# Third layer's edge phase: sigmoid and its products with the edge scalar issued one step sooner, second features in a ring of four buffers

## Chip, cores and metric

The kernel runs on one core of one Trainium2 chip. The metric is the device time of one execution in microseconds (us). Before the change it took 13953.59 us as the median of three runs (13917.46 to 13966.27).

## What is computed

Four graph-network layers over 6250 nodes and 100000 edges, float32 throughout. The change lies in the edge phase of the third layer (`_L2_gnn_ref` of the reference). Cut to what matters, with `s` for 64 scalars and `v` for 32 three-vectors of an edge:

```python
w1 = rbf @ W_rbf
m1_s, m1_v = _cg_tp(msg_s, msg_v, y0, y1, *split(w1))   # messages: products with y0, y1
a = sum(leaky(m1_s @ W_alpha) * alpha_dot)               # attention logit
val_s, val_v = m1_s @ Ws_val, einsum(m1_v, Wv_val)
val_v = val_v * sigmoid(val_s @ Wg)[..., None]           # gate
val_s = sigmoid(val_s)
m2_s, m2_v = _cg_tp(val_s, val_v, y0, y1, w2...)         # second product: val_s*y0, dot(val_v, y1), ...
hs, hv = m2_s @ Ws_vlin, einsum(m2_v, Wv_vlin)           # stored per edge
```

`_cg_tp` multiplies scalars by the edge scalar `y0` and by the edge vector `y1`, and takes the dot and cross products of vectors with `y1`.

## The kernel before

The edges are padded to 784 columns of 128. `layer2_edges` (L1917) works on items of four columns (TM = 4, 512 edges), 196 items in all (NM). All engines run the same software pipeline: `steps` (L84) calls a body per step n, and the body handles item n - s for each stage number s. The first and last steps are written out and the middle is a loop over four unrolled steps. The order on each engine is the order of the code, and engines meet only by semaphores. The stages are named in L1918:

- Stage 0: SyncE loads indices and edge features, GpSimd gathers eight blocks of rows (`pool_gather`, L731): four of `gs`, then four of `gd`.
- JOIN 1, PRODUCT 2: VectorE adds `gs` and `gd` to `msg` (L2095) and forms the first features `F` (`dve_message_products`, L629). Its instruction at L644 waits until the four quarters of the item that had this `F` buffer before have been transposed; `F` has two buffers.
- TURN 3: TensorE transposes each of the four quarters of `F` (L677), ScalarE copies them to `FT` (L707), TensorE multiplies by the weights (L658 to L660) and ScalarE copies the result to `O` (L713). The multiplication follows its transposes by two quarters.
- CROSS 5: VectorE finishes the attention logit and the cross product in `O`.
- SECOND_IN 6: ScalarE takes the sigmoid of 96 columns of `O` into the second features `F2` (L1993) at the head of its step, and multiplies 64 of them by `y0`, a quarter at a time, as the last ScalarE instruction of each of the four quarters of that step (`sigmoids_y0`, L1983). The fourth one raises `second_in`. VectorE multiplies the vectors by the gate (L2090) and forms the dot product (L2108, L2123).
- TURN2 7: TensorE transposes `F2` (L677, two blocks a quarter), ScalarE copies to `FT2` (L707, 256 columns), TensorE multiplies (L698, L699), ScalarE copies to `O2` (L720, L721), one of the two with a factor `y0`. For this path there is one PSUM buffer for the transposes and one for the products, so the transposes of a quarter wait until ScalarE has copied those of the quarter before.
- CROSS2 9, LAST 10: VectorE adds the second cross product (L596), SyncE stores.

On each quarter k ScalarE's order is: FT, O, FT2, O2, product with `y0`. TensorE's order is: three transposes, the first multiplication, two transposes of `F2`, the second multiplication; after quarter 1 come the eight matmuls of the edge weights (L2038). At the head of a step TensorE waits, before any of its work:

```python
if m := i_of(TURN):
    wait_apart(pe, sem("products"), m[0] + 1, passed)
if m := i_of(TURN2):
    wait_apart(pe, sem("products2"), m[0] + 1, passed)
    wait_apart(pe, sem("second_in"), m[0] + 1, passed)
```

Since SECOND_IN is 6 and TURN2 is 7, the `second_in` that TensorE's step n + 1 needs is raised by the last ScalarE instruction of step n. `F2` has two buffers, and `prod`, `dot` and `lk` are scratch arrays of VectorE.

Of the kernel before, what the change touches and what calls it, by code (L numbers as in the profile page):

```python
# [585 lines left out]
def comp(ap, n=3):  # L586

    return ap.rearrange("p t (d c) -> p t d c", d=n)
# [1327 lines left out]

def layer2_edges(nc, W, D, logits):  # L1917
    JOIN, PRODUCT, TURN, CROSS, SECOND_IN, TURN2, CROSS2, LAST = 1, 2, 3, 5, 6, 7, 9, 10  # L1918
    RING = 4
    with ExitStack() as ctx:  # L1920
        S = Names(nc, ctx, "e2")
# [7 lines left out]
        ix = [S.sb(f"ix{u}", [P, 2, TM], I32) for u in range(2)]  # L1929
        gs, gd, msg = pair("gs", [P, TM, CX]), pair("gd", [P, TM, CX]), S.sb("msg", [P, TM, MSG_W])  # L1930
        nine = S.sb("nine", [P, TM, NINE_W])
        prod, dot = S.sb("prod", [P, TM, C1V]), S.sb("dot", [P, TM, C1])
        F, F2 = pair("F", [P, TM, X_W]), pair("F2", [P, TM, F2_W + C1])
        FT, FT2 = S.sb("FT", [P, TM, X_W]), S.sb("FT2", [P, TM, F2_W])
        tmp = S.sb("tmp", [P, 3, TM, C1V])
        LIN, VEC, O_W, O2_W = 160, 164, 292, 288
        O, O2 = ([S.sb(f"{name}{u}", [P, TM, w]) for u in range(RING)] for name, w in (("O", O_W), ("O2", O2_W)))
        lk, lsum = S.sb("lk", [P, TM, 64]), S.sb("lsum", [P, TM, 4])
        psW, psF, psO = S.ps("psW", [P, TM, 256]), S.ps("psF", [P, 3, 512]), S.ps("psO", [P, 3, 512])
        parts = ((F[0], 384), (F[1], 384), (F2[0], ET - 768))  # L1940
        starts = (0, 384, 768)
# [35 lines left out]
        @block.scalar  # L1977
        def _(act):
            act.wait_ge(sem("y"), 2 * len(parts))

            def times_y0(to, src, i, k):

                return nc.scalar.activation(to[:, k, :], src[:, k, :], ACT.Copy, scale=y0_of(i, k))  # L1983

            def body(i_of_ring):
                i_of = by_two(i_of_ring)

                def sigmoids():
                    if m := i_of_ring(SECOND_IN):
                        i, u, j = m  # L1990
                        act.wait_ge(sem("lin_O"), (i + 1) * TM)
                        wait(act, sem("lin2_turned"), (i - 1) * TM)
                        nc.scalar.activation(F2[u % 2][:, :, F_B:F_B + C0 + C1], O[u][:, :, 64:160], ACT.Sigmoid).then_inc(sem("sig"), 1)  # L1993

                def sigmoids_y0(k):
                    if m := i_of(SECOND_IN):
                        i, u, j = m
                        if k == 0:
                            act.wait_ge(sem("sig"), i + 1)
                        done = times_y0(F2[u][:, :, F_A:F_A + C0], F2[u][:, :, F_B:F_B + C0], i, k)  # L2000
                        if k == TM - 1:
                            done.then_inc(sem("second_in"), 1)

                sigmoids()
                for k in range(TM):
                    if m := i_of(TURN):
                        act_move(nc, act, m[0], k, FT, psF[:, k % 2, :], S, "lin")
                    if m := two_behind(i_of_ring, TURN, k):
                        i, u, j, n = m
                        if n == 0:  # L2010
                            wait(act, sem("gated"), i - RING + 1)
                            wait(act, sem("logit"), i - RING + 1)
                        act_result(nc, act, i, n, O[u], psO[:, n % 2, :], O_W, S, "lin")
                    if m := i_of(TURN2):
                        act_move(nc, act, m[0], k, FT2, psF[:, 2, :], S, "lin2", F2_W)
                    if m := two_behind(i_of_ring, TURN2, k):
                        i, u, j, n = m
                        if n == 0:
                            wait(act, sem(f"stored{u}"), j * 16)
                        act_result_y0(nc, act, i, n, O2[u], psO[:, 2, :], y0_of(i, n), S, "lin2")  # L2020
                    sigmoids_y0(k)

            steps(act, NM, LAST, body, RING)

        @block.tensor
        def _(pe):
            passed = sem("pe_passed")

            def body(i_of_ring):
                i_of = by_two(i_of_ring)  # L2030

                def weights():
                    if m := i_of(JOIN):
                        i, u, j = m
                        wait_apart(pe, sem(f"es{u}"), (j + 1) * 32, passed)
                        wait_apart(pe, sem("products"), i, passed)
                        for k in range(TM):
                            last = nc.tensor.matmul(psW[:, k, 0:224], es[u][:, P * k:P * k + P], W["l2_rbf"][:, :], start=True, stop=True)  # L2038
                        last.then_inc(sem("weights"), 1)
# [6 lines that stand above are left out]
                for k in range(TM):  # L2046
                    if m := i_of(TURN):
                        i, u, j = m
                        pe_turn(nc, pe, i, k, F[u], psF[:, k % 2, :], W["ident"], S, "lin", 2)
                    if m := two_behind(i_of, TURN, k):  # L2050
                        i, u, j, n = m
                        pe_message_maps(nc, pe, i, n, FT, psO[:, n % 2, :], W, "l2", 96, S, "lin", 2)
                    if m := i_of(TURN2):
                        i, u, j = m
                        pe_turn(nc, pe, i, k, F2[u], psF[:, 2, :], W["ident"], S, "lin2", 1, 2)
                    if m := two_behind(i_of, TURN2, k):
                        i, u, j, n = m
                        pe_maps_y0(nc, pe, i, n, FT2, psO[:, 2, :], W, S, "lin2", 1)
                    if k == 1:
                        weights()  # L2060
# [5 lines left out]
        def _(dve):  # L2066
# [10 lines left out]
            def body(i_of_ring):  # L2077
                i_of = by_two(i_of_ring)
                if m := i_of(PRODUCT):
                    i, u, j = m  # L2080
                    wait(dve, sem("products"), i)
                    dve_message_products(nc, dve, i, psW, msg, nine, dot, F[u], Y3(i), S, (sem("lin_turned"), (i - 1) * TM))
                if m := i_of(SECOND_IN):

                    i, u, j = m
                    dve.wait_ge(sem("sig"), i + 1)
                    dve.wait_ge(sem("cross_done"), i + 1)
                    wait(dve, sem("lin2_turned"), (i - 1) * TM)
                    V2 = comp(F2[u][:, :, F2_X:F2_X + C1V])
                    tt(V2, comp(O[i_of_ring(SECOND_IN)[1]][:, :, VEC:VEC + C1V]), bcast(F2[u][:, :, F2_W:F2_W + C1], 2, 3), ALU.mult).then_inc(sem("gated"), 1)  # L2090
                if m := i_of(JOIN):
                    i, u, j = m
                    dve.wait_ge(sem(f"gathered{u}"), (j + 1) * 16 * 2 * TM)
# [2 lines left out]
                if m := i_of_ring(CROSS):  # L2096
# [4 lines left out]
                    a = O[u][:, :, 0:64]  # L2101
                    nc.vector.scalar_tensor_tensor(out=lk[:, :, :], in0=a, scalar=0.0, in1=bcast(W["l2_adot"][:, :], 1, TM), op0=ALU.max,
                                                   op1=ALU.mult).then_inc(sem("leaky"), 1)
                if m := i_of(SECOND_IN):
                    i, u, j = m
                    dve.wait_ge(sem("gated"), i + 1)
                    wait(dve, sem("products2"), i)
# [1 line left out]
                if m := i_of_ring(CROSS):  # L2109
# [7 lines left out]
                        .then_inc(sem("summed"), 1)  # L2117
                    dve.wait_ge(sem("cross_first"), i + 1)
                    tt(C, C, comp(tmp[:, 0, :, :]), ALU.add).then_inc(sem("cross_done"), 1)
                if m := i_of(SECOND_IN):  # L2120
                    i, u, j = m
                    dve.wait_ge(sem("prod2"), i + 1)
                    nc.vector.tensor_reduce(F2[u][:, :, F_D:F_D + C1], prod[:, :, :].rearrange("p t (d c) -> p t c d", d=3), AX.X,  # L2123
# [712 lines left out]
```

## Time and profile before

| | us |
|---|---|
| median of three runs | 13953.59 |
| profiled execution, its own time | 13971.56 |
| its span (first to last instruction) | 13969.8 |
| the edge phase of the third layer | 8094 to 11145 of the span |

Step times are starts in microseconds from the span's start. A row of the timeline gives start, duration, engine, line, operation, the tiles (names without their buffer number: `e_F` stands for `F` and `F2`, `e_O` for `O` and `O2`, `e_FT` for `FT` and `FT2`), and in brackets the idle time ahead of it and what ended it. The releaser's name is inferred from the semaphore's number, which several layers share. Some rows of ScalarE and VectorE in this phase name a DMA or a tile of another layer as releaser; the wait in the code is on TensorE there.

### The profile page before, as it was taken

How to read it: one execution, taken by the hardware profiler on the slowest of the kernel's cores; microseconds unless marked ns; L12 is line 12 of the kernel's file. 1: busy time of each engine (PE TensorE's matmuls, PEld its weight loads, DVE VectorE, ACT ScalarE, POOL GpSimd, SP SyncE). 2: the span in 40 equal slices, each digit the busy share in tenths (PEclk: the TensorE clock that was granted, in tenths of full speed). 3: DMA queues.
4: the chain of work that ended last, by engine and by line, in shares of the span. 5: the costliest groups of instructions: out<-in, count | busy, mean ns of one | idle time of the engine just before them, and what ended most of it. 6: DMA issues, size and time to landing. Idle time of an engine off the chain costs nothing. (4 is left out here: it accounts for less than half of the span.)

```text
span 13969.8 us, 239951 instructions
## 1 busy us (share of the span) xinstructions
PE 10808.1 (77%) x55109; PEld 9201.4 (66%) x55109; DVE 8552.1 (61%) x21245; ACT 4566.3 (33%) x11584; POOL 8205.8 (59%) x8212
## 2 busy tenths in 40 slices
PE   2988888856658999999999457777777656788885
PEld 2888888845556777777777456666666645555564
DVE  4677777789634444444444467777777796566663
ACT  1444444430122222222222235555555501233331
POOL 4777777748625555555655255555555375566660
PEclk7777777768756666666666678888888787788995
DMA  3443444437403333333333322222222274233321
GB/s 91 92 91 91 91 92 92 92 104 207 118 14 65 62 62 63 61 63 61 64 61 61 96 66 67 69 69 69 69 68 68 58 191 128 70 82 82 83 81 45
DMA packets 1350653, 1138.02 MB, mean 81 GB/s; under 512 B 558798, under 2 KB 1147331, under 8 KB 1349895
## 3 DMA queue, kind: packets, MB, share of 16 engines
q0 software_dynamic: 347904, 478.51, 18.0%
q1 hardware_dynamic: 854716, 549.77, 14.3%
q10 hardware_dynamic: 147914, 108.40, 3.0%
q8 instruction: 45, 0.74, 0.0%
q14 instruction: 74, 0.60, 0.0%
HBM read 767.61 MB, written 368.33 MB: 81 GB/s over the span
## 5 line engine op out<-in xcount | busy, mean ns | idle before, releaser
L738 POOL DMA_INDIRECT e_gs<-tab_src,e_ix x1568 | 1680.4, 1072 | 1264.9 <-DVE e_msg L2095 801.6
L677 PE MATMUL e_psF<-w_ident,e_F 128*128 128x128 f32 x6272 | 1395.9, 335 | 756.3 <-ACT e_F L1983 504.7
L738 POOL DMA_INDIRECT e_gd<-tab_dst,e_ix x1568 | 1667.6, 1064 | 477.8 <-issue 473.5
L789 POOL DMA_INDIRECT acc<-e_sums,e_row x784 | 1249.9, 1594 | 1183.5 <-ACT e_sums L1687 1044.4
L677 PEld LDWEIGHTS e_psF<-w_ident,e_F 128*128 128x128 f32 x6272 | 950.8, 180 | 928.6 <-issue 882.3
L707 ACT ACTIVATE e_FT<-e_psF 128x384 f32<-128x384 f32 (+1 forms) x2352 | 1067.6, 454 | 914.2 <-PE e_psF L677 569.4
L1801 POOL DMA_INDIRECT e_g<-tab_src,e_er x976 | 993.3, 1018 | 609.9 <-DVE e_rows L1897 322.0
L1627 PEld LDWEIGHTS e_psS<-e_same,e_rows 128*128 128x128 f32 x6272 | 1129.9, 275 | 313.6 <-issue 310.7
L1627 PE MATMUL e_psS<-e_same,e_rows 128*128 128x128 f32 x6272 | 1248.0, 371 | 1.2 <-DVE e_same L763 1.2
L713 ACT ACTIVATE e_O<-e_psO 128x352 f32<-128x352 f32 (+1 forms) x1568 | 688.1, 439 | 961.7 <-PE e_psO L660 271.7
L1563 PE MATMUL s_psS<-s_wv,s_hot 128*128 128x168 f32 (+1 forms) x3904 | 669.7, 315 | 412.6 <-POOL s_wv L1521 213.7
L738 POOL DMA_INDIRECT e_g<-tab_src,e_ix x784 | 841.8, 1074 | 248.5 <-issue 202.9
L1563 PEld LDWEIGHTS s_psS<-s_wv,s_hot 128*128 128x128 f32 x3904 | 562.6, 191 | 519.4 <-issue 297.1
L1637 PE MATMUL e_psP<-w_l_out_v,e_turned 128*128 128x32 f32 x4704 | 876.4, 334 | 0.0
L1637 PEld LDWEIGHTS e_psP<-w_l_out_v,e_turned 128*128 128x128 f32 x4704 | 872.8, 271 | 0.0
L1682 ACT ACTIVATE e_turned<-e_psS 128x512 f32<-128x512 f32 x784 | 467.4, 596 | 986.6 <-PE e_psS L1627 900.9
L1839 PE MATMUL e_psS<-e_rows,e_hot 128*128 128x384 f32 x1952 | 771.9, 542 | 8.6 <-issue 5.7
L1713 DVE TENSOR_TENSOR e_prod<-e_g,e_dirs 128x384 f32<-128x384 f32 x196 | 109.5, 559 | 1080.7 <-DMA e_g<-tab_src,e_ix 1032.3
L1687 ACT ACTIVATE e_sums<-e_psP 128x192 f32<-128x192 f32 x784 | 258.8, 330 | 1389.5 <-PE e_psP L1637 1168.1
L1635 PE MATMUL e_psP<-w_l_out_s,e_turned 96*128 96x96 f32 x1568 | 419.7, 361 | 310.7 <-ACT e_sums L1687 310.7
L2294 POOL TENSOR_TENSOR n_st<-n_st,w_half 128x8 f32<-128x8 f32 x70 | 113.4, 1637 | 884.6 <-DVE n_st L2718 739.0
L1660 PE MATMUL e_psW<-w_l_fc,e_h 64*128 64x224 f32 x1568 | 619.5, 569 | 1.4 <-ACT e_h L1675 1.4
(492 smaller groups left out, 27261.0 us busy)
## 6 DMA issues: line engine op xcount, KB each, us to landing
val<-e_O SPq DMA_DIRECT2D x392, 320.0 KB
s_val<-val ACTq DMA_DIRECT2D x244, 320.0 KB, 3.3
s_val<-val SPq DMA_DIRECT2D x244, 320.0 KB
e_krow<-in_src_t SPq DMA_DIRECT2D x196, 256.0 KB
sums<-e_total SPq DMA_DIRECT2D x244, 192.0 KB
e_es<-in_es SPq DMA_DIRECT2D x196, 130.0 KB
e_gs<-tab_src,e_ix POOLq DMA_INDIRECT x1568
e_gd<-tab_dst,e_ix POOLq DMA_INDIRECT x1568
```

The lines of the kernel that those rows point to most:

```text
L677: last = nc.tensor.transpose(psF[:, P * g:P * g + P], F[:, k, P * g:P * g + P], ident[:, :])
L707: nc.scalar.activation(FT[:, k, :], psF[:, 0:width], ACT.Copy).then_inc(S.sem(tag + "_FT"), 1)
L713: nc.scalar.activation(O[:, k, :], o[:, 0:width], ACT.Copy).then_inc(S.sem(tag + "_O"), 1)
L738: pool.indirect_dma_start(into[t][u][:, k, :], None, tables[t], bass.IndirectOffsetOnAxis(ix[u][:, t, k:k + 1], 0))\
L789: pool.indirect_dma_start(acc[k], bass.IndirectOffsetOnAxis(T["row"][u][:, k:k + 1], 0), T["sums"][u][:, k, :], None, compute_op=ALU.add). ...
L1563: last = nc.tensor.matmul(psS[u % HALF][:, 0:width], hot[u % HALF][:, k, :], wv[u % HALF][:, k, :], start=(k == 0), stop=(k == TM - 1))
L1627: last = nc.tensor.matmul(psS[:, k % 2, P * c:P * c + P], rows[u][:, k, P * c:P * c + P], T["same"][u][:, k, :], start=True, stop=True, sk ...
L1637: last = nc.tensor.matmul(o[:, 96 + C1 * d:96 + C1 * d + C1], f[:, P * d + P:P * d + 2 * P], W["l1_out_v"][:, :], start=True, stop=True, s ...
L1660: last = nc.tensor.matmul(psWs[u][:, k, 0:wn], h[u][:, P * k:P * k + P], W["l1_fc2"][:, :], start=True, stop=True)
L1682: nc.scalar.activation(turned[k % 2][:, :], psS[:, k % 2, :], ACT.Copy).then_inc(sem("moved"), 1)
L1801: pool.indirect_dma_start(g[u % ROWS4][:, k, :], None, D["tab_src"], bass.IndirectOffsetOnAxis(er[u][:, k, 12:13].bitcast(I32), 0))\
L1839: last = nc.tensor.matmul(psS[u % 2][:, 0:width], hot[u % 2][:, k, :], rows[u % 2][:, k, :], start=(k == 0), stop=(k == TM - 1))
```

## The change

The sigmoid and its products with `y0` get a stage number of their own, SIGMOID = CROSS = 5. VectorE's gate and dot product stay at 6 and TensorE's transposes of `F2` at 7. `F2` becomes a ring of four, indexed by the item modulo four. To make room, `prod`, `dot` and `lk` become views into `W["norm"]`, two arrays of 784 columns whose contents the first two layers used up.

```diff
+    SIGMOID = CROSS
...
-        prod, dot = S.sb("prod", [P, TM, C1V]), S.sb("dot", [P, TM, C1])
-        F, F2 = pair("F", [P, TM, X_W]), pair("F2", [P, TM, F2_W + C1])
+        spare = lambda n, a, c: W["norm"][n][:, a:a + TM * c].rearrange("p (t c) -> p t c", c=c)
+        prod, dot, lk = spare(0, 0, C1V), spare(1, 0, C1), spare(1, TM * C1, 64)
+        F = pair("F", [P, TM, X_W])
+        F2 = [S.sb(f"F2{u}", [P, TM, F2_W + C1]) for u in range(RING)]
...
                 def sigmoids():
-                    if m := i_of_ring(SECOND_IN):
+                    if m := i_of_ring(SIGMOID):
                         i, u, j = m
                         act.wait_ge(sem("lin_O"), (i + 1) * TM)
-                        wait(act, sem("lin2_turned"), (i - 1) * TM)
-                        nc.scalar.activation(F2[u % 2][:, :, F_B:F_B + C0 + C1], O[u][:, :, 64:160], ACT.Sigmoid).then_inc(sem("sig"), 1)
+                        wait(act, sem("lin2_turned"), (i - RING + 1) * TM)
+                        nc.scalar.activation(F2[u][:, :, F_B:F_B + C0 + C1], O[u][:, :, 64:160], ACT.Sigmoid).then_inc(sem("sig"), 1)
 
                 def sigmoids_y0(k):
-                    if m := i_of(SECOND_IN):
+                    if m := i_of_ring(SIGMOID):
...
-                    if m := i_of(TURN2):
+                    if m := i_of_ring(TURN2):
                         i, u, j = m
                         pe_turn(nc, pe, i, k, F2[u], psF[:, 2, :], W["ident"], S, "lin2", 1, 2)
...
-                if m := i_of(SECOND_IN):
+                if m := i_of_ring(SECOND_IN):
 
                     i, u, j = m
                     dve.wait_ge(sem("sig"), i + 1)
                     dve.wait_ge(sem("cross_done"), i + 1)
-                    wait(dve, sem("lin2_turned"), (i - 1) * TM)
+                    wait(dve, sem("lin2_turned"), (i - RING + 1) * TM)
```

In the loop no instruction changes its place on its engine; what changes is the item that it works on. The first place is ScalarE in the second of the four unrolled steps, quarter 0 (`e2_O3` is buffer 3 of `O`, `e2_F21` buffer 1 of `F2`; ISA and REGISTER_ALU rows are address registers). Before:

```order
L1993 ACTIVATE e2_F21<-e2_O3 128x4x96
L705 ISA
L707 ACTIVATE e2_FT<-e2_psF 128x384
L713 ACTIVATE e2_O1<-e2_psO 128x292
L707 ACTIVATE e2_FT2<-e2_psF 128x256
L720 ACTIVATE e2_O21<-e2_psO 128x2x96
L721 ISA
L721 ACTIVATE e2_O21<-e2_psO,e2_y 128x96
L1983 ISA
L1983 ACTIVATE e2_F21<-e2_F21,e2_y 128x64
```

The same step now:

```order
L1996 ACTIVATE e2_F20<-e2_O0 128x4x96
L705 ISA
L707 ACTIVATE e2_FT<-e2_psF 128x384
L713 ACTIVATE e2_O1<-e2_psO 128x292
L705 ISA
L707 ACTIVATE e2_FT2<-e2_psF 128x256
L720 ACTIVATE e2_O21<-e2_psO 128x2x96
L721 ISA
L721 ACTIVATE e2_O21<-e2_psO,e2_y 128x96
```

The sigmoid takes `O` buffer 0, the next item after buffer 3, at the same place; one address-register row more stands ahead of the FT2 copy.

The second place is TensorE in the same step, quarter 0, before:

```order
L677 MATMUL e2_psF<-w_ident,e2_F0 128x128 x3
L78 REGISTER_ALU
L658 MATMUL e2_psO<-w_l2_t0,e2_FT 128x164
L659 MATMUL e2_psO<-w_l2_t1,e2_FT 128x128
L660 MATMUL e2_psO<-w_l2_t2,e2_FT 128x96
L78 REGISTER_ALU
L677 MATMUL e2_psF<-w_ident,e2_F20 128x128 x2
```

and now:

```order
L677 MATMUL e2_psF<-w_ident,e2_F0 128x128 x3
L78 REGISTER_ALU
L658 MATMUL e2_psO<-w_l2_t0,e2_FT 128x164
L659 MATMUL e2_psO<-w_l2_t1,e2_FT 128x128
L660 MATMUL e2_psO<-w_l2_t2,e2_FT 128x96
L78 REGISTER_ALU
L677 MATMUL e2_psF<-w_ident,e2_F22 128x128 x2
```

The order is the same. Before, ScalarE filled buffer 1 of `F2` while TensorE read buffer 0, the item just ahead of it; now ScalarE fills buffer 0 while TensorE reads buffer 2, two items ahead. One item, filled in the step between, lies finished.

## Rows read from the trace of the kernel before

**Rows 1.** The page, 40 equal slices of the span (349 us each), granted TensorE clock in tenths.

```profile
PEclk7777777768756666666666678888888787788995
```

**Rows 2.** Stretches of the span: busy time by engine, granted clock, DMA share, GB/s.

```profile
8310.00:11050.00 2740.00, 2036.91 (x12074) 1855.34 (x12072) 2016.59 (x4436) 1448.32 (x4441) 1570.00 (x1421) 0.83 0.27 68
...
12100.00:13400.00 1300.00, 1155.56 (x4794) 776.13 (x4792) 847.20 (x1911) 407.53 (x1146) 828.45 (x959) 0.89 0.30 82
```

**Rows 3.** Two source lines of ScalarE, the sigmoid and the products, with who waited.

```profile
L1993 ACT ACTIVATE e_F<-e_O x196: 511/539/594, 8161.5 to 11117.9; 128x384 f32<-128x384 f32 x196
...
  DVE e_F L2090: 297.5, 165
...
L1983 ACT ACTIVATE e_F<-e_F,e_y x784: 338/347/423, 8162.6 to 11126.4; 128x64 f32<-128x64 f32 x196
...
  PE e_psF L677: 504.7, 169
```

**Rows 4.** Groups of instructions, 8310 to 11050 us: busy, mean ns, idle before, releasers.

```profile
L738 POOL DMA_INDIRECT e_gs<-tab_src,e_ix x709 | 793.1, 1119 | 950.8 <-DVE e_msg L2095 758.8 <-issue 192.0
...
L738 POOL DMA_INDIRECT e_gd<-tab_dst,e_ix x712 | 776.9, 1091 | 216.9 <-issue 216.9
...
L644 DVE TENSOR_TENSOR e_F<-e_psW,e_msg 128x512 f32<-128x512 f32 x178 | 123.1, 691 | 370.7 <-DMA acc<-e_sums,e_row 333.3 <-issue 25.1 <-PE e_psF L677 12.0
...
L2090 DVE TENSOR_TENSOR e_F<-e_O,e_F 128x384 f32<-128x384 f32 x177 | 98.8, 558 | 325.6 <-ACT e_F L1993 279.8 <-issue 45.8
```

**Rows 5.** Timeline of ScalarE, one step and the joints at both its ends.

```profile
9505.89 0.54 ACT L1993 ACTIVATE e_F<-e_O 128x384 f32<-128x384 f32 x1
...
9508.93 0.38 ACT L707 ACTIVATE e_FT<-e_psF 128x256 f32<-128x256 f32 x1
...
9511.92 0.33 ACT L720 ACTIVATE e_O<-e_psO 128x192 f32<-128x192 f32 x1
...
9515.20 0.49 ACT L707 ACTIVATE e_FT<-e_psF 128x384 f32<-128x384 f32 x1 [2.49 <-PE e_psF L677]
...
9515.88 0.39 ACT L707 ACTIVATE e_FT<-e_psF 128x256 f32<-128x256 f32 x1
...
9516.15 0.35 ACT L720 ACTIVATE e_O<-e_psO 128x192 f32<-128x192 f32 x1
...
9520.43 0.38 ACT L707 ACTIVATE e_FT<-e_psF 128x256 f32<-128x256 f32 x1 [1.03 <-remote]
9520.71 0.33 ACT L720 ACTIVATE e_O<-e_psO 128x192 f32<-128x192 f32 x1
...
9521.14 0.36 ACT L1983 ACTIVATE e_F<-e_F,e_y 128x64 f32<-128x64 f32 x1
9521.38 0.53 ACT L1993 ACTIVATE e_F<-e_O 128x384 f32<-128x384 f32 x1
...
9524.65 0.38 ACT L707 ACTIVATE e_FT<-e_psF 128x256 f32<-128x256 f32 x1
```

**Rows 6.** Timeline of TensorE over the same step and into the next.

```profile
9511.81 1.78 PE L2038 MATMUL e_psW<-w_l_rbf,e_es 32*128 32x224 f32 x8
9513.52 0.55 PE L677 MATMUL e_psF<-w_ident,e_F 128*128 128x128 f32 x3
...
9515.32 0.49 PE L677 MATMUL e_psF<-w_ident,e_F 128*128 128x128 f32 x3
...
9517.16 0.44 PE L699 MATMUL e_psO<-w_l2b_t,e_FT 128*128 128x160 f32 x2
9521.89 0.87 PE L677 MATMUL e_psF<-w_ident,e_F 128*128 128x128 f32 x3 [4.29 <-ACT e_F L1983]
...
9525.29 0.85 PE L677 MATMUL e_psF<-w_ident,e_F 128*128 128x128 f32 x3
```

**Rows 7.** Two stretches around that joint: columns as in Rows 2.

```profile
9510.30:9520.50 10.20, 7.26 (x51) 6.29 (x50) 7.62 (x18) 4.87 (x17) 7.48 (x7) 1.00 0.38 101
9520.50:9527.30 6.80, 5.41 (x25) 5.40 (x26) 5.36 (x13) 3.91 (x12) 2.64 (x3) 0.50 0.08 19
```

More of the change, by code:

```diff
@@ L1937, in layer2_edges @@
         O, O2 = ([S.sb(f"{name}{u}", [P, TM, w]) for u in range(RING)] for name, w in (("O", O_W), ("O2", O2_W)))
-        lk, lsum = S.sb("lk", [P, TM, 64]), S.sb("lsum", [P, TM, 4])
+        lsum = S.sb("lsum", [P, TM, 4])
         psW, psF, psO = S.ps("psW", [P, TM, 256]), S.ps("psF", [P, 3, 512]), S.ps("psO", [P, 3, 512])
@@ L2087, in body @@
                     dve.wait_ge(sem("cross_done"), i + 1)
-                    wait(dve, sem("lin2_turned"), (i - 1) * TM)
+                    wait(dve, sem("lin2_turned"), (i - RING + 1) * TM)
                     V2 = comp(F2[u][:, :, F2_X:F2_X + C1V])
-                    tt(V2, comp(O[i_of_ring(SECOND_IN)[1]][:, :, VEC:VEC + C1V]), bcast(F2[u][:, :, F2_W:F2_W + C1], 2, 3), ALU.mult).then_inc(sem("gated"), 1)
+                    tt(V2, comp(O[u][:, :, VEC:VEC + C1V]), bcast(F2[u][:, :, F2_W:F2_W + C1], 2, 3), ALU.mult).then_inc(sem("gated"), 1)
                 if m := i_of(JOIN):
@@ L2103, in body @@
                                                    op1=ALU.mult).then_inc(sem("leaky"), 1)
-                if m := i_of(SECOND_IN):
+                if m := i_of_ring(SECOND_IN):
                     i, u, j = m
@@ L2119, in body @@
                     tt(C, C, comp(tmp[:, 0, :, :]), ALU.add).then_inc(sem("cross_done"), 1)
-                if m := i_of(SECOND_IN):
+                if m := i_of_ring(SECOND_IN):
                     i, u, j = m
```

## The prediction, made before any run of the change

> **What bounds the kernel now.** I read the slices of the page first, then stretches of the span, then the source lines that the change moves, and last the timeline of one step, engine by engine. The slices show TensorE's granted clock at seven or eight tenths over slices 24 to 32, where this phase lies [rows 1]. No slice is at ten, so the clock falls again and again inside the phase.
>
> The stretch from 8310 to 11050 us is the phase without its ramps. It holds 178 steps (the count of L644 there), so a step takes 2740 / 178 = **15.39 us** [rows 2, 4]. No engine is full in it: VectorE is busy 2016.59 / 178 = 11.33 us a step, TensorE 11.44 us. GpSimd is busy 1570.00 us and its issue idles are 192.0 + 216.9 us, together 11.12 us a step; what remains of its idle time, 758.8 us, is for VectorE's `msg` [rows 2, 4]. The phase is therefore a loop of waits, and the lines show which: TensorE waited 169 times, 504.7 us in all, about 3.0 us each, for the last product with `y0`, and VectorE 165 times, 297.5 us, for the sigmoid [rows 3].
>
> The timeline shows the loop at one joint. TensorE's last matmul of the step is recorded as over at 9517.16 + 0.44 = 9517.60. ScalarE copies the transposes of quarter 3 at 9520.43, the product at 9520.71, multiplies by `y0` from 9521.14 to 9521.50, and TensorE's first transpose of the next step follows at 9521.89 after 4.29 us of idleness [rows 5, 6]. From the last product that ScalarE waited for (9520.71) to the restart are 1.18 us in which TensorE owes nobody anything. The restart is slow: quarter 0 takes 9525.29 - 9521.89 = 3.40 us, against 15.32 - 13.52 = 1.80 us for quarter 2 [rows 6], and the granted clock is 0.50 (1.2 GHz) around the restart and 1.00 (2.4 GHz) in the stretch before it, whose last three microseconds were idle [rows 7, 6].
>
> One thing in the rows warns against a simple sum. ScalarE's copy of quarter 3's transposes begins at 9520.43 and that of its product at 9520.71, 3.1 us after TensorE's recorded end; in quarter 2 the copy of the first transposes starts at 9515.20, 1.1 us after their recorded end at 9514.07 [rows 5, 6]. At 2.4 GHz, matmuls are usable later than their rows say. The Trainium skill ("Perfetto Trace Analysis", Tensor Engine Instruction) says that the end of a matmul in a profile is estimated and that the semaphore goes out when PSUM has acknowledged the data; the trace agrees in kind, with its 3.1 us. I take ScalarE's starts, not TensorE's ends, as the time of a result.
>
> **The change part by part.**
>
> *The wait at the head of TensorE's step.* `second_in` for the item is now raised a whole step before it is needed, 15.39 us earlier. The other two waits there have the same slack as before: `products` and `products2` come from VectorE's previous step. After its last matmul TensorE can go on at once with the three transposes and the first multiplication of the next quarter 0, since their inputs and buffers are free since quarter 2. It then stops at the transposes of `F2`, which need ScalarE's copy of quarter 3 (9520.43 + 0.38 = 9520.81), and at the second multiplication, which needs the PSUM buffer that ScalarE reads from 9520.71 on. So ScalarE's order sets the joint: copy, product with `y0`, sigmoid, and then FT, O, FT2 of quarter 0 with no waiting. The sigmoid ends at 9521.38 + 0.53 = 9521.91. From the FT copy to the FT2 copy of a quarter whose inputs are ready are 9515.88 - 9515.20 = 0.68 us. The FT2 copy of quarter 0 can start at 9522.59, and it started at 9524.65: a gain of 2.06 us. At the joint before, the same sum is 9505.89 + 0.54 + 0.68 = 9507.11 against 9508.93: 1.82 us [rows 5]. The mean is **1.94 us a joint**. TensorE transposes both kinds of features in 192 steps, and two of these I leave out for the ramps: 190 joints, 190 x 1.94 = 369 us.
>
> Its bounds. Below: if results of TensorE come only as fast as they come now, just the 1.18 us in which it owed nothing can be won, and nothing at all or a loss if the missing rest makes its results later still (a rival below). Above: a step cannot be shorter than VectorE's 11.33 us of work, a gain of 4.06 us, 771 us in all. I take 1.94, the nearest row-for-row sum, since all it needs is that results of nine small matmuls issued up to 3 us early are there when ScalarE comes to them.
>
> *The sigmoid.* VectorE no longer waits for it at L2090 (297.5 us) [rows 3]. This is worth nothing by itself: VectorE has 4.06 us of slack a step, and what it loses less here it waits more at L644, whose releaser is TensorE's quarter 3 [rows 4, 2]. Without this cover it would be 1.7 us a step. Its `msg` comes a little earlier in the step, so GpSimd's gathers start earlier; at 11.12 us they fit into a step of 13.45 us.
>
> *ScalarE.* The same instructions in the same places, plus a few address-register rows. It is busy 1448.32 / 178 = 8.1 us a step [rows 2], and what hides these rows is its idle time; at the joint they could cost at most some hundredths of a microsecond. *Scratch in `norm`, ring of four:* no instruction more or less on VectorE or TensorE, the same shapes; nothing. If the ring's address work were exposed it would be in the same hundredths. SyncE's and GpSimd's queues are not touched.
>
> *The clock.* TensorE's recorded pause shrinks from 4.29 us to about 2.5 us: nine of the fifteen matmuls of a quarter, 9/15 x 1.80 = 1.1 us, follow 9517.60 at once, up to 9518.7, and the rest can follow the copy's end, 9520.81, as the restart followed the last product with `y0`, by 9521.89 - 9521.50 = 0.39 us, at 9521.2. Whether the granted clock then stays at 2.4 GHz the trace cannot say. The forecast takes it as it is now and puts the rest in a rival. The Trainium skill ("TensorE: Matmul & The Clock Gate", HAM oscillation) holds that idle gaps in every iteration bring the clock down each time and that closing them keeps it up; rows 7 agree for the long gap, and by that rule alone the result would be the second rival's. [...]
>
> **Sum.** 13971.6 (the profiled execution) - 369 = 13603 us; the median of the runs lies 18 us below the profiled execution, so **13585 us**.
>
> **The rivals.**
>
> 1. *Results of TensorE are the limit* (gain 0.3 to 1.3 us a joint). For it: the 3.1 us between recorded and usable results. Then quarter 0's early matmuls are late as well and only the 1.18 us are won: 190 x 1.18 = 224 us, 13730 us. Against it: quarter 0 after a rest shows no such lateness.
> 2. *The clock stays up* and quarter 0 runs like quarter 2: another 3.40 - 1.80 = 1.60 us, a step of 15.39 - 1.94 - 1.60 = 11.85 us, close above VectorE's 11.33. 190 x 3.54 = 673 us, 13281 us; at VectorE's floor 13183. For it: in a later phase (12100 to 13400 us) the clock is 0.89 with TensorE busy 1155.56 of 1300 us [rows 2]. Against it: a pause of 2.5 us remains.
> 3. *Nothing changes*: TensorE waits as long behind quarter 0's FT2 as it did at the head, because the copies of quarter 3 come later by what TensorE started earlier. 13954 us. Against it: ScalarE's idle time at the joint would have to grow again by 1.94 us.
> 4. *Slower: the rest was useful.* The place is TensorE's quarters at 2.4 GHz. Quarter 3 took 9520.71 - 9516.15 = 4.56 us by ScalarE's copies [rows 5], more than quarter 0's 3.40 us at 1.2 GHz after its rest. If without rest all quarters slow down, a step is four quarters plus 9513.52 - 9511.81 = 1.71 us of edge weights [rows 6]; it is longer than 15.39 from 3.42 us a quarter on. Halfway between 3.40 and 4.56, at 3.98, it is 17.63 us: 190 x 2.24 = 426 us more, 14362 us. Against it: quarter 2 with the edge weights took only 9516.15 - 9511.92 = 4.23 us together.
>
> That the change does not do what it says is part of rival 3: the semaphore counts and the buffers read show that TensorE reads an item two behind ScalarE's, so I give it next to nothing.
>
> **How the numbers follow.** Forecast (gain 1.3 to 2.6 us, 13460 to 13707 us) 0.40; rival 1, 0.20; rival 2, 0.24; rival 3, 0.08; rival 4, 0.08. About 0.3%, 42 us or 0.22 us a joint, is what a measurement of this kernel can tell from none. Faster 0.84, same 0.08, slower 0.08. The range must leave out rivals 3 and 4 (0.16) and may leave out 0.04 of rival 2's far side: from 13290 (a gain of 3.5 us) to 13900 us (0.3 us).
>
> **What would show it.** TensorE's wait for L1983 and VectorE's for L1993 vanish from the waits; TensorE's first matmul of a step follows its last within 0.5 us, and its longest wait moves to the transposes of `F2` in quarter 0, behind L707. VectorE's wait at L644 grows or stays. The stretch of 178 steps takes 2395 us. The clock stays near 0.83 by the forecast, goes above 0.9 by rival 2. The forecast is wrong if the step stays above 14.3 us, or if ScalarE's copies of quarter 0 wait for TensorE as long as they do now.

## The result, and the profile after

| | before | changed |
|---|---|---|
| median, us | 13959.93 (13917.46 to 13992.57, 4 runs) | 13817.97 (13772.74 to 13828.43, 4 runs) |
| profiled execution, span, us | 13969.8 | 13771.0 |
| mean granted clock of the profiled execution | 0.747 | 0.748 |
| third layer's edges, first to last start of the message sum, us | 2984.8 | 2837.5 |

The ratio is 0.9894, interval 0.9858 to 0.9929: 142 us faster, where 369 were forecast. Measured again in another set of runs: 13794.40 against 13949.75 us, 0.9893 (0.9877 to 0.991). In two of the later sets of runs the kernel before took only 11742.80 and 11752.58 us (one run each), and in a third, on the chip of the latter, 13949.75 us again, so each experiment is read beside the kernel before of its own set.

The lines below are those of the changed kernel, 3 higher than before from the sigmoid on. First the steady stretch, with the columns of [rows 2]:

```profile
8290.00:10900.00 2610.00, 2073.78 (x12155) 1822.87 (x12156) 2014.04 (x4478) 1389.74 (x4475) 1583.23 (x1428) 0.83 0.28 72
```

It holds 179 steps: 2610 / 179 = 14.58 us, where 13.45 were forecast from 15.39. That is above the 14.3 us which the prediction had named as the sign of being wrong. The granted clock is 0.83 as before. The sigmoid and the products, which answer to [rows 3], have no row any more under those who wait:

```profile
L1996 ACT ACTIVATE e_F<-e_O x179: 518/538/598, 8296.2 to 10893.2; 128x384 f32<-128x384 f32 x179
...
who waited for it (us, times):
...
L1986 ACT ACTIVATE e_F<-e_F,e_y x716: 346/348/472, 8291.8 to 10898.0; 128x64 f32<-128x64 f32 x179
...
who waited for it (us, times):
```

Both waits are gone, 504.7 and 297.5 us by [rows 3], and the phase is 147 us shorter. TensorE now goes on at the joint at once: its pause there was 2.9 us on average over the 172 middle steps before (items 12 to 183 of 196), and is 0.14 us now, never more than 0.67. What stands in their place are waits that are rarer and far longer; engine, tensor, line, what it waited for, us in total, times, the longest:

```profile
PEld e_psF L677 <- issue: 470.0, 513, 6.8
POOL e_gs L738 <- DVE e_msg L2098: 389.3, 83, 15.2
DVE e_F L644 <- PE e_psF L677: 302.7, 47, 15.9
ACT e_FT L707 <- PE e_psF L677: 282.6, 169, 4.2
...
PE e_psF L677 <- ACT e_FT L707: 222.9, 132, 4.9
```

The last of these was, in the kernel before:

```profile
PE e_psF L677 <- ACT e_FT L707: 31.0, 40, 1.9
```

VectorE's idle time before L644, the same group as in [rows 4], is 570.1 us now:

```profile
L644 DVE TENSOR_TENSOR e_F<-e_psW,e_msg 128x512 f32<-128x512 f32 x179 | 123.4, 689 | 570.1 <-PE e_psF L677 302.7 <-DMA acc<-e_sums,e_row 253.8 <-issue 13.5
```

VectorE waits 47 times, up to 15.9 us, for TensorE. The steps are no longer alike. Of the 172 middle ones 53 take 11.2 to 11.6 us by the distance of the message sums, VectorE's floor, and 56 take 16 us or more, the longest 27.3; before, all lay between 12.7 and 17.4 us. The timeline of one such stretch shows why. TensorE first, then ScalarE, which copies TensorE's results:

```profile
8475.81 0.36 PE L660 MATMUL e_psO<-w_l_t,e_FT 128*128 128x96 f32 x2
8476.69 0.41 PE L677 MATMUL e_psF<-w_ident,e_F 128*128 128x128 f32 x2 [0.52 <-ACT e_FT L707]
8477.70 0.46 PE L698 MATMUL e_psO<-w_l2b_t,e_FT 128*128 128x128 f32 x2 [0.60 <-issue]
...
8481.14 0.41 PE L677 MATMUL e_psF<-w_ident,e_F 128*128 128x128 f32 x2 [1.19 <-ACT e_FT L707]
```

```profile
8479.19 0.41 ACT L713 ACTIVATE e_O<-e_psO 128x292 f32<-128x292 f32 x1 [1.02 <-DMA s_pb<-probs]
8480.61 0.38 ACT L707 ACTIVATE e_FT<-e_psF 128x256 f32<-128x256 f32 x1 [1.01 <-remote]
```

The product that L713 copies is recorded as over at 8475.81 + 0.36 = 8476.17. ScalarE is free from 8478.17 on and copies it only at 8479.19, 3.0 us after that end. The transposes recorded as over at 8476.69 + 0.41 = 8477.10 are copied at 8480.61, 3.5 us later. The names behind the arrows (a DMA of a tensor of another phase, "remote") are guesses of the profile.

This is quarter 3 of a step, where the prediction had seen such lateness too. Whether it belongs to that place is told by all the copies of L713 in the middle steps before which ScalarE had stood idle, for more than 0.03 us: the lateness is the copy's start less the recorded end of the last L660 matmul of what it copies. Copies more than 0.5 us late, of those that waited:

| | quarter 0 | quarter 1 | quarter 2 | quarter 3 | latest, us |
|---|---|---|---|---|---|
| before | 0 of 166 | 0 of 140 | 94 of 130 | 124 of 124 | 5.6 |
| changed | 40 of 84 | 53 of 77 | 76 of 130 | 49 of 64 | 15.0 |

In the kernel before, the two quarters after the pause are free of lateness and the last two are not. In the changed kernel, which has no pause, it is met in all four. Its latest copy is in quarter 0:

```profile
10292.26 0.36 PE L660 MATMUL e_psO<-w_l_t,e_FT 128*128 128x96 f32 x2
```

```profile
10307.59 0.41 ACT L713 ACTIVATE e_O<-e_psO 128x292 f32<-128x292 f32 x1 [2.36 <-DMA s_pb<-probs]
```

### The profile page after: what moved, and what is told of

It reads as the page before. It is cut to its first block and busy times, and to the rows that moved or that the text cites. A ratio compares the mean times of both kernels' runs of the same rounds, so it can differ in the third digit from the quotient of the medians.

```text
span 13771.0 us, 240219 instructions
## 1 busy us (share of the span) xinstructions
PE 10809.3 (78%) x55109; PEld 9131.5 (66%) x55109; DVE 8524.9 (62%) x21245; ACT 4493.7 (33%) x11584; POOL 8227.1 (60%) x8212
## 5 line engine op out<-in xcount | busy, mean ns | idle before, releaser
L677 PE MATMUL e_psF<-w_ident,e_F 128*128 128x128 f32 x6272 | 1354.3, 327 | 465.2 <-ACT e_FT L707 308.0
L707 ACT ACTIVATE e_FT<-e_psF 128x384 f32<-128x384 f32 (+1 forms) x2352 | 1088.8, 463 | 848.3 <-PE e_psF L677 367.2
L677 PEld LDWEIGHTS e_psF<-w_ident,e_F 128*128 128x128 f32 x6272 | 912.8, 174 | 646.4 <-issue 594.0
L713 ACT ACTIVATE e_O<-e_psO 128x352 f32<-128x352 f32 (+1 forms) x1568 | 697.7, 445 | 942.3 <-PE e_psO L660 245.9
L1635 PEld LDWEIGHTS e_psP<-w_l_out_s,e_turned 96*128 96x128 f32 x1568 | 326.2, 258 | 446.6 <-issue 443.7
```

Source lines behind the costliest of these rows:

```text
L677: last = nc.tensor.transpose(psF[:, P * g:P * g + P], F[:, k, P * g:P * g + P], ident[:, :])
L707: nc.scalar.activation(FT[:, k, :], psF[:, 0:width], ACT.Copy).then_inc(S.sem(tag + "_FT"), 1)
L713: nc.scalar.activation(O[:, k, :], o[:, 0:width], ACT.Copy).then_inc(S.sem(tag + "_O"), 1)
L1635: nc.tensor.matmul(o[:, 0:96], f[0:96, 0:P], W["l1_out_s"][:, :], start=True, stop=True, skip_group_check=True)
```

## The experiments

The length of the phase is that from the first to the last start of VectorE's message sum, 195 steps, read from that line's row in each kernel; lines move by a few from kernel to kernel. It is one profile's: two profiles of the changed kernel differ by 5.7 us (f1 below). Lateness is counted as in the table above, in the 172 middle steps. Each kernel from e3 on, other than e4, e10 and f1, leaves part of the gathered node features out or takes other rows.

**Which part of the change is worth what.** e1 keeps ring and scratch and takes back the move; e2 moves the sigmoid alone.

The first edit is e1's, the second e2's.

```diff
-    SIGMOID = CROSS
+    SIGMOID = SECOND_IN
```

```diff
                 def sigmoids_y0(k):
-                    if m := i_of_ring(SIGMOID):
+                    if m := i_of_ring(SECOND_IN):
```

> The ring of four and the scratch in norm stay, the sigmoid and its products go back to the stage of VectorE's gate. Theory (the gain comes from TensorE's wait for the last product with y0, which was served a step late): the wait is back at every joint, about 500 us in the waits over the stretch of 178 steps, a step of 15.4 us, and the whole takes 13960 us, as before. Rival (the second pair of buffers by itself loosens the loop): the time stays near 13820 us.

> Only the sigmoid is a step sooner; its four products with y0 stay one step later. Theory: VectorE's wait for the sigmoid vanishes, TensorE's wait for the last product stays, a step of 15.4 us, 13960 us in all. Rival (VectorE's earlier gate, and with it earlier gathers, is what gained): 13820 us.

```profile
L2098 DVE TENSOR_TENSOR e_msg<-e_gs,e_gd x196: 815/818/826, 8096.5 to 11087.5; 128x640 f32<-128x640 f32 x196
```

```profile
L2098 DVE TENSOR_TENSOR e_msg<-e_gs,e_gd x196: 811/815/832, 8083.5 to 11006.0; 128x640 f32<-128x640 f32 x196
```

e1 (first row): 2991.0 us, 13936.26 us in all, ratio 0.9986 (0.9972 to 1.0001): ring and scratch are worth nothing that can be measured, and TensorE's wait for the last product is back, 438.2 us between 8310 and 11050 us. e2 (second row): 2922.5 us, 13885.53 us, 0.9938 (0.9918 to 0.9959), with TensorE still waiting for the last product, 348.5 us between 8310 and 11050 us. So the sigmoid alone gives 62 us of the phase's 147 (70 us between the medians), and the products of `y0` the other 85. The sigmoid was to be worth nothing. e2 lies between its two expected times, and whether it gains by VectorE's own wait or by the earlier gathers is not told apart.

**Gathers, or TensorE's stream.** If late results of TensorE, made by GpSimd's gathers, bound the step, e3 must shorten it; if the number of TensorE's instructions does, e4 must lengthen it. e3 leaves TensorE, VectorE and ScalarE as they are and takes away six of eight gathers; e4 puts sixteen more semaphore increments a step, four in each quarter, into TensorE's stream.

```diff
-                    pool_gather(nc, pool, *m, ix, (D["tab_src"], D["tab_dst"]), (gs, gd), S, (sem("msg"), m[0] - 1))
...
+                    for t in range(2):
+                        pool.indirect_dma_start((gs, gd)[t][u][:, 0, :], None, (D["tab_src"], D["tab_dst"])[t],
+                                                bass.IndirectOffsetOnAxis(ix[u][:, t, 0:1], 0)).then_inc(sem(f"gathered{u}"), 16)
```

```diff
+                    for _ in range(4):
+                        pe.sem_inc(passed, 1)
```

> The changed kernel, but GpSimd gathers only the first of the four quarters of each item (two gathers a step in place of eight); the other quarters hold rows loaded once ahead of the phase. In the changed kernel a step takes 14.6 us and TensorE's results come up to several us after their rows. Theory A (the gathers make them late): the step falls to VectorE's floor of about 11.5 us, the whole by 190 x 3.1 = 590 us to about 13190 us. Theory B (the lateness has nothing to do with gathers): the step stays between 14 and 15 us, 13750 to 13850 us.

> The changed kernel with four more semaphore increments in TensorE's queue in each quarter, 16 a step, no more work for its array. Theory C (TensorE's queue is bound by the number of its instructions, some 180 a step): the step grows by about 9 percent, 14.6 to 15.9 us, the whole by 250 us to 14070 us. If the lateness has another cause: the step stays at 14.6 us, 13820 us.

e3 took 13111.79 us, 2167.6 us for the phase. Its waits between 8300 and 10300 us:

```profile
POOL e_gs L1983 <- DVE e_msg L2107: 1491.9, 171, 9.0
ACT e_FT L707 <- PE e_psF L677: 505.4, 173, 5.6
...
PE e_psW L2049 <- DVE e_F L649: 205.0, 143, 2.3
ACT e_O L713 <- PE e_psO L660: 92.0, 203, 0.9
```

Nobody waits for more than 0.9 us for the product of L660. The up to 5.6 us at L707 are for transposes that TensorE has not begun; it waits for VectorE itself, at L2049. No copy of L713 comes more than 0.12 us after its recorded end. VectorE waits for another engine once, 2.4 us: the phase is 2167.6 / 195 = 11.12 us a step with its ramps, and the middle steps take 11.28 us, of which VectorE is busy 11.12. e4 took 13900.66 us, with 99 us of phase more than the changed kernel: the increments cost 0.51 us a step, where 1.3 were expected if their number bound it, so TensorE's stream matters too. It is not what the 670 us of e3 are, for e3 leaves that stream as it is.

**What of the gathers.** All of these start from the changed kernel. e5 keeps eight gathers a step, of 16 bytes a row; e6 loads as many bytes by eight plain transfers of SyncE and leaves GpSimd idle.

```diff
+                        for k in range(TM):
+                            pool.indirect_dma_start(small[u][:, t, k, :], None, (D["small_src"], D["small_dst"])[t],
+                                                    bass.IndirectOffsetOnAxis(ix[u][:, t, k:k + 1], 0)).then_inc(sem(f"gathered{u}"), 16)
...
+    D["small_src"], D["small_dst"] = dram("small_src", (NPAD, 4)), dram("small_dst", (NPAD, 4))
```

```diff
+                            sp.dma_start((gs, gd)[t][u][:, k, :], (D["tab_src"], D["tab_dst"])[t][P * (TM * t + k):P * (TM * t + k) + P, :])\
+                                .then_inc(sem(f"gathered{u}"), 16)
...
-                    pool_gather(nc, pool, *m, ix, (D["tab_src"], D["tab_dst"]), (gs, gd), S, (sem("msg"), m[0] - 1))
```

> Edit, on the changed kernel: GpSimd issues its eight gathers a step as before, but each row gathered is 16 bytes instead of 640, from small tables; the two operands of the message sum are loaded once ahead of the loop, so the gathered node features are left out of the computation. The instructions of GpSimd and the number of row descriptors stay, the bytes go to a fortieth. Before it: the changed kernel took 14.63 us a step, and with two full gathers a step instead of eight (e3) 11.28 us, with ScalarE's copies starting soon after TensorE's recorded ends. If the bytes of the gathers make TensorE's results late, the step goes to 11.3 to 11.6 us (about 13120 us in all). If it is their number (GpSimd making descriptors, the queue carrying them), the late results stay: step 14 to 14.7 us, about 13650 to 13780 us.

> Edit, on the changed kernel: the eight gathers a step are replaced by eight loads of the same 2.6 MB-wide shape each (128 rows of 640 bytes, contiguous rows of the tables), issued by SyncE, with the same wait for the message buffer; GpSimd does nothing in the phase and no indices are loaded, so the node features taken are those of the wrong rows. The bytes that land stay, the software queue goes. If the bytes matter: step 14 to 14.7 us, about 13650 to 13780 us. If GpSimd's making of descriptors matters: step 11.3 to 11.6 us, about 13120 us, and ScalarE's copies within 0.5 us of TensorE's recorded ends.

(A load or gather of 128 rows of 640 bytes is 82 kB; the 2.6 MB in the expectation are a slip.) e5 took 13858.15 us (phase 2861.0) and had copies up to 13.0 us late, e6 13116.55 us (phase 2168.5) and none above 0.12. So it is not the bytes. In e6 the pair of rows from above reads

```profile
8472.91 0.58 PE L660 MATMUL e_psO<-w_l_t,e_FT 128*128 128x96 f32 x2
```

```profile
8473.61 0.41 ACT L713 ACTIVATE e_O<-e_psO 128x292 f32<-128x292 f32 x1 [0.86 <-PE e_psO L660]
```

which is 0.12 us from the recorded end (8473.49) to the copy, against 3.0 us. These matmuls ran at the lower clock. A pair of the same step at the higher one, by the matmuls' length, is 0.03 us apart. So the prediction's "At 2.4 GHz, matmuls are usable later than their rows say" is no matter of the clock alone:

```profile
8478.05 0.36 PE L660 MATMUL e_psO<-w_l_t,e_FT 128*128 128x96 f32 x2
```

```profile
8478.44 0.41 ACT L713 ACTIVATE e_O<-e_psO 128x292 f32<-128x292 f32 x1 [0.20 <-PE e_psO L660]
```

Then the number of gathers, the number of rows and GpSimd's being busy. The edits to e3's and e6's text: four gathers (`for k in range(2)`), eight gathers of 32 rows (`[u][0:32, k, :]`, indices `[0:32]`), and in e6 twenty fills of a scratch array of 512 columns on GpSimd. They ran twice, first as

> Edit, on the changed kernel: four gathers a step instead of eight; the other two quarters of both message operands are loaded once ahead, so half of the gathered node features is left out. Eight gathers a step gave 14.63 us a step, two 11.28 us (e3). If lateness grows in proportion to the number of gathers, the step is 12.4 us (11.28 plus a third of 3.35 us), about 13330 us in all. If it comes only when GpSimd's queue is nearly full (eight gathers take 8.9 us of its time in a step), it is not there at four: 11.3 us, about 13110 us.

> Edit, on the changed kernel with plain loads (e6): GpSimd now also fills a scratch array of 512 columns twenty times a step, after the wait for the message buffer, so that it is busy for about as long as with its eight gathers, without any gather. As in e6 the node features are those of the wrong rows. If GpSimd's being busy is what makes TensorE's results late, the step goes back to 14 to 14.7 us, about 13700 us in all. If it is the gathers as such, it stays at e6's 11.3 us, about 13117 us.

> Edit, on the changed kernel: eight gathers a step, each of 32 rows instead of 128 (rows of 640 bytes as before); the other partitions of both message operands are loaded once ahead, so three quarters of the gathered node features are left out. The number of gathers stays, the number of gathered rows is that of e3 (256 a step). If the number of gather instructions (with their sixteen increments each) makes the results late, the step stays at 14 to 14.7 us, about 13700 us in all. If it is the number of rows, it is 11.3 to 11.6 us, about 13120 us.

beside a kernel before of 11752.58 us. There all three had phases at VectorE's floor (2177.6, 2167.7 and 2201.6 us; 11676.59, 12042.96 and 11704.20 us in all, e13's fills outlasting the phase), and in none was a copy of L713 more than 0.12 us late. So they do not tell which property of the gathers matters. They tell that eight gathers a step alone are not enough, and that the lateness is not a fixed property of a kernel. They ran again beside the changed kernel itself:

> The changed kernel as it is. On a chip where the kernel before takes about 13950 us: 13818 us within 0.3%, as measured. On a chip where the kernel before takes about 11750 us: if the late results made the joint that the change removes, both kernels run the third layer's edges at VectorE's floor there (11.3 us a step) and the ratio is 1.000 within 0.003; if the joint of 1.94 us a step were real without them, the changed kernel would be 369 us faster there, ratio 0.969.

> The kernel of e7 again, for which the chip of that call had no late results. Where the kernel before takes about 13950 us: in proportion to the number of gathers 12.4 us a step, about 13330 us; only at a nearly full queue 11.3 us, about 13110 us. Where it takes about 11750 us: 11.3 us a step, as in e7.

> The kernel of e13 again. The phase of the third layer's edges alone is to be read, since GpSimd's twenty fills a step (13.9 us) outlast it: 2168 us and 11.3 us a step if GpSimd's being busy does nothing to TensorE's results, 14 to 14.7 us a step if it is what makes them late.

> The kernel of e14 again. Where the kernel before takes about 13950 us: 14 to 14.7 us a step (about 13700 us) if the number of gather instructions makes the results late, 11.3 to 11.6 us (about 13120 us) if it is the number of gathered rows. Where it takes about 11750 us: 11.3 us, as in e14.

This time, on the same chip, the kernel before took 13949.75 us and f1 13794.40 us (phase 2843.2, copies up to 10.7 us late). The rows of the message sum in f2, f3 and f4, in this order:

```profile
L2108 DVE TENSOR_TENSOR e_msg<-e_gs,e_gd x196: 807/816/859, 8068.9 to 10248.8; 128x640 f32<-128x640 f32 x196
```

```profile
L2105 DVE TENSOR_TENSOR e_msg<-e_gs,e_gd x196: 760/816/826, 8121.2 to 10289.5; 128x640 f32<-128x640 f32 x196
```

```profile
L2108 DVE TENSOR_TENSOR e_msg<-e_gs,e_gd x196: 806/816/891, 8073.2 to 10954.1; 128x640 f32<-128x640 f32 x196
```

f3: 2168.4 us with GpSimd busy 1547.44 of the 2000 us from 8300 on, more than with its gathers in f1 (1219.45), and no copy over 0.12 us late: it is not GpSimd's being busy. In all it took 13569.18 us, its fills outlasting the phase. f4: 2880.9 us (13830.58 in all), copies up to 11.2 us late, as slow as full gathers with a quarter of the rows. With e5 this leaves the number of gather instructions, not their rows or bytes. f2: 2179.9 us (13128.13 in all), 11.18 us a step with four gathers, though 49 copies are over 0.5 us late, up to 2.1 us, and ScalarE's longest wait for L660 is 1.8 us, against 0.9 in e3. The row of f2, and that of the kernel before from 8310 to 11050 us:

```profile
ACT e_O L713 <- PE e_psO L660: 92.5, 227, 1.8
```

```profile
ACT e_O L713 <- PE e_psO L660: 247.6, 351, 1.8
```

So some results are late at four gathers as well, and the step still absorbs it; at eight it does not.

**The change without late results.** e9 makes e3's edit on the kernel before.

> Edit, on the kernel before: two gathers a step instead of eight (the other three quarters of both message operands are loaded once ahead of the loop, so three quarters of the gathered node features are left out), as e3 did on the changed kernel. It tells what the change is worth where TensorE's results are not late. My prediction's joint (1.94 us a step) stands if this kernel keeps the joint: step about 13.2 us or more (11.28 of e3 plus 1.94), some 13480 us in all, with TensorE waiting for y0's last product at L1983. If the late results also made the joint what it was, the step falls to VectorE's floor here too, 11.3 us, about 13110 us, and the change is worth nothing without them.

It took 13072.04 us. TensorE's wait for the last product, line 1991 there, the steady part of the phase and the row of the sum:

```profile
  PE e_psF L677: 209.2, 170
```

```profile
8300.00:10300.00 2000.00, 1667.40 (x11696) 1520.46 (x11694) 1953.90 (x4366) 1359.93 (x4331) 372.65 (x334) 0.94 0.18 49
```

```profile
L2104 DVE TENSOR_TENSOR e_msg<-e_gs,e_gd x196: 809/816/827, 8027.2 to 10194.7; 128x640 f32<-128x640 f32 x196
```

TensorE still waits for the product in the old order, 209.2 / 170 = 1.23 us a step where [rows 3] had 3.0. But the phase takes 2167.5 us, e3's 2167.6, and no copy is more than 0.12 us late. Where results are in time, TensorE's pause at the joint is still there, but fits beside VectorE's work, and its removal is worth nothing. The last three kernels were to fill in four and six gathers.

> Edit, on the kernel before: four gathers a step instead of eight, as f2 did on the changed kernel (half of the gathered node features is left out). f2 had results up to 3.2 us late and still a step of 11.33 us. If late results are what TensorE's wait for y0's last product consists of, some of it shows here: the path from TensorE over ScalarE back to TensorE, which the change opens, has no slack in the kernel before, so the step is 11.8 to 13 us, 13200 to 13450 us in all, and the change is worth that much at four gathers. If the change only helps once the whole step is disturbed, it is 11.33 us here too, about 13110 us.

> Edit, on the changed kernel: six gathers a step (a quarter of the gathered node features is left out). Steps of 11.28, 11.33 and 14.65 us were measured with two, four and eight. If the cost is in proportion beyond four gathers: 13.0 us, about 13460 us in all. If it sets in only at a nearly full queue: 11.3 to 11.6 us, about 13130 us.

> Edit, on the kernel before: six gathers a step. With e9 (two) 11.29 us and 15.41 with eight. In proportion: 14.0 us, about 13660 us in all, so that the change is worth 1 us a step at six gathers. With a threshold near eight: as g1.

They met a kernel before of 11742.80 us, so how the worth of the change grows with the lateness stays open. g1: 11681.66 us, phase 2176.8. For six gathers, the changed order (g2) took 11700.57 us, phase 2186.9, the old one (g3) 11708.62 us, phase 2187.5: with nothing late, the two are the same, as e3 and e9 say. The changed kernel with all its eight gathers was not run beside a kernel before of 11750 us; the nearest is e14, with eight gathers of 32 rows.

**A version with more slack for GpSimd.** e10 puts the index buffers of the changed kernel in a ring of four.

```diff
-        ix = [S.sb(f"ix{u}", [P, 2, TM], I32) for u in range(2)]
+        ix = [S.sb(f"ix{u}", [P, 2, TM], I32) for u in range(RING)]
```

> Edit, on the changed kernel: the index buffers are in a ring of four instead of two, so that SyncE loads the indices of a step two steps earlier. In the changed kernel GpSimd waited 205 us of the steady stretch for indices (33 times) and 389 us for the message buffers. If GpSimd's lateness in one step is what makes the irregular steps of 16 to 20 us, this takes up to 205 us off: 13600 to 13750 us. If TensorE's late results bound the step, GpSimd only waits for the message buffers instead: within 0.3% of 13818 us.

13789.84 us, ratio 0.987 (0.9847 to 0.9893), phase 2840.3 us against 2837.5. GpSimd's wait for indices is gone and the one for the message buffers grew:

```profile
POOL e_gs L738 <- DVE e_msg L2100: 438.5, 85, 15.1
```

The interval overlaps that of the change alone, so this is no measured gain. No kernel here that leaves nothing out is measurably faster than the change.

## Why the prediction was right and wrong

- *The direction and the vanished waits* were right. The wait for the last product and that for the sigmoid are gone, TensorE's first matmul follows its last within 0.5 us in 141 of the 172 middle steps, and its wait moved behind L707 (31.0 to 222.9 us); VectorE's idle time at L644 grew from 370.7 us [rows 4] to 570.1.
- *The floor.* That a step cannot be shorter than VectorE's work holds. The 11.33 us were slightly too much: in e3, e6, e9 and f3 the middle steps take 11.28 to 11.29 us, with VectorE busy 11.12 to 11.13 of them.
- *The step that failed is the 1.94 us a joint.* It was to be 190 x 1.94 = 369 us. Measured: 147.3 us over 195 steps, **0.76 us** a step. The sum took ScalarE's starts as the time of a result, and then asked "that results of nine small matmuls issued up to 3 us early are there when ScalarE comes to them". They are not: of the changed kernel's 355 copies of L713 that waited, 218 come more than 0.5 us after the recorded end, up to 15.0 us. The sum treated the 3.1 us at the joint as a price of that one place, and left quarters 0 and 1 without any, because they had none before. Before, they came behind TensorE's pause; without it they are late in 93 of 161 waits. e9 shows how much of the pause was lateness: without it TensorE waits 1.23 us there, not 3.0.
- *Rival 1*, that TensorE's results are the limit, is what happened; it had 0.20 where the forecast had 0.40. Its window of 0.3 to 1.3 us holds the 0.76. Its own term, 1.18 us and 224 us, was still half as large again as what was measured: it has quarter 0's results late as well, which they are, but not later than before. That they may come "later still" without the rest stands at the range's lower bound, without a price. What spoke against rival 1, that quarter 0 shows no lateness after a rest, is true of all 166 waits there in the kernel before. It was no evidence, since the change takes the rest away. The count of waits would not have warned either: e9, where nothing is late, waits 365 times at L713, but for 127.9 us and at most 0.9 us, against 351 times, 247.6 us and 1.8 us before.
- *Rival 4*, that the rest was useful, has part of the mechanism: quarters 0 and 1 are late without it. As the phase became shorter all the same, that loss is smaller than what the closed joint gave. (Its 14362 us should read 13954 + 426 = 14380; nothing else rests on it.)
- *The sigmoid was priced at nothing* because VectorE has slack on average. e2 gives 62 us for it. In a mean over steps slack of 4.06 us covers a wait of 1.7; in a phase whose late results fall on some steps and not on others, the wait adds to the late ones. That last sentence is argued from the uneven steps; no run isolates it.
- *Ring and scratch at nothing* was right, by e1 within 0.3%: ratio 0.9986.
- *The clock* was left as it is, and stayed (0.83). Rival 2's clock does rise once nothing is late: 0.94 in e9, 0.91 in e6. There the step lies at VectorE's floor, so that the clock does not set it; what the 0.83 costs a step of 14.58 us, no run isolates. By the rule quoted from the Trainium skill ("TensorE: Matmul & The Clock Gate", HAM oscillation) closing the gaps of every iteration keeps the clock up; here one gap was closed and others opened (TensorE's wait behind L707 from 31.0 to 222.9 us), so the runs do not contradict it.
- *GpSimd fits into the step* was true of its busy time and missed its role: its waits for the message buffers fell from 758.8 us [rows 4] to 389.3, while 205.1 us of waits for indices came new. It is by their number that its gathers make TensorE's results late.

## What to carry to other kernels

If an engine's results are usable later than their rows say, find out first at which places and on what it depends, by taking the suspected traffic away on the kernel before. Ask of a pause that is to be closed whether the work behind it is in time only because of it. Price a removed wait against steps without the disturbance as well: here it was worth nothing without late results, and 0.76 of an expected 1.94 us with them. And take a step's mean slack as cover only where the steps are alike.

## What the runs showed of the hardware

- Beside a kernel before of about 13950 us, eight gathers a step from GpSimd make results of TensorE usable long after their recorded ends: copies of L713 that waited come up to 5.6 us late in the kernel before and up to 15.0 us in the changed one. With plain loads of the same bytes (e6), with two gathers (e3, e9) and with twenty fills of GpSimd in place of gathers (f3) none comes later than 0.12 us; with four gathers (f2) 49 come over 0.5 us late, up to 2.1. Rows of 16 bytes (e5, up to 13.0 us) or a quarter of the rows (f4, up to 11.2 us) do not help. The cost in this phase is 2837.5 - 2167.6 = 670 us. By which path a gather reaches TensorE's results, and whether the result is late or only its signal, no run shows.
- After a pause of TensorE of 2.9 us on average the lateness is gone: in the kernel before none of 306 waiting copies in quarters 0 and 1 is over 0.5 us late, and 218 of 254 in quarters 2 and 3 are.
- One and the same chip ran the kernel before in 11752.58 us in one set of runs and in 13949.75 us (median) in another. In the first, four gathers took 2177.6 us for the phase with no copy over 0.12 us late; in the second 2179.9 us with copies up to 2.1 us late. Eight gathers of 32 rows took 2201.6 us, none over 0.12 us late, against 2880.9 us and up to 11.2. What differed around the chip is not in any trace and stays open. The Trainium skill ("NOTIFIC — the notification-queue block", Overflow: three behaviours, one of which stalls the engine) says that the block that takes the engines' records makes them wait rather than lose a record inside it; no run here shows whether that is at work.
- Sixteen more semaphore increments a step on TensorE cost 0.51 us a step (e4).
